# Scales of the weights spread over three other elements of distance attention; its last element interleaved with ratio attention's first tile

## The reference

```
# 1: distance attention, 16 heads of 16, 257 keys for each batch element
scores = Q K^T / 4 - slope[head] * (query_pos - key_pos);  masked: -inf
e = exp(scores - max);  attn = e / (1 + sum(e));  x = x + (attn V) W_o
# 2: ratio attention among the 32 tokens of an element, causal
dot = q k^T;  scores = dot^2 / (|q|^2 + |k|^2 - 2 dot + 1e-6)
x = x + softmax(scores) v w_out + b_out
# 3: feed-forward on weights rounded to 4 bits, in blocks of 32:
s = max(max|w_block| / 7, 1e-12);  w = clip(round(w / s)) * s
```

## Time and profile before

| | us |
|---|---|
| median of 3 runs | 744.56 (742.48 to 746.54) |
| the profiled execution | 744.72 |
| its span, first to last instruction | 742.9 |
| mean granted TensorE clock in it | 0.934 of full speed |

### The profile page before, as it was taken

How to read it: one execution, slowest core, us unless ns; L and a number is a source line. 1 busy time by engine, 2 the same in 40 slices (tenths; PEclk the granted TensorE clock), 3 DMA queues, 4 the chain that set the end, 5 groups by cost and what they waited for, 6 DMA issues and landing times.

```text
span 742.9 us, 18871 instructions
## 1 busy us (share of the span) xinstructions
PE 640.5 (86%) x7075; PEld 482.5 (65%) x7075; DVE 467.4 (63%) x1335; ACT 367.0 (49%) x992; POOL 311.5 (42%) x458
## 2 busy tenths in 40 slices
PE   4779999999989699986985899988999776999990
PEld 3557777877766578753434687667887573777760
DVE  1577766776776568874398864558878875333330
ACT  1445646655655569754486642336666431222320
POOL 1316655656632469720000030136565513556641
PEclk9889999999999889977997799999999986999995
DMA  8623332333310000039100525438001022243434
GB/s 266 225 58 87 88 78 72 89 82 81 88 36 3 2 3 4 4 96 336 51 1 0 213 71 226 173 131 366 3 3 65 3 100 53 46 70 59 66 44 71
DMA packets 31705, 65.21 MB, mean 88 GB/s; under 512 B 5792, under 2 KB 21792, under 8 KB 29312
## 3 DMA queue, kind: packets, MB, share of 16 engines
q1 hardware_dynamic: 26016, 55.73, 22.9%
q0 software_dynamic: 4688, 7.18, 5.9%
q10 hardware_dynamic: 912, 1.10, 0.4%
HBM read 57.67 MB, written 7.37 MB: 88 GB/s over the span
## 4 chain that ended last, share of the span: by engine, by line
PE 60%; DVE 23%; issue 5%; ACT 5%; DMA 2%; SPq 2%; POOL 0%; DVEq 0%; ACTq 0%; POOLq 0%
PE psum L2649 7%; PE psum L491 7%; PE psum L483 4%; PE psum L2659 4%; PE psum L516 4%; PE psum L1504 3%; PE psum L1481 3%; PE psum L859 3%; DVE ff_peak L1522 2%; DVE s_sb L659 2%; PE psum L868 2%; PE psum L851 2%; PE psum L505 2%; PE psum L899 2%; DMA wn<-in_w_down 2%
## 5 line engine op out<-in xcount | busy, mean ns | idle before, releaser
L804 POOL TENSOR_SCALAR bias<-dist,cst 128x257 f32<-128x257 f32 x128 | 59.8, 486 | 83.0 <-DVE dist L650 64.1
L659 DVE CUSTOM_DVE_ANT_0 s_sb<-psum,bias 128x257 f32<-128x257 f32 x128 | 46.9, 423 | 39.5 <-PE psum L505 37.5
L422 ACT ACTIVATE prob<-s_sb,negm 128x257 f32<-128x257 f32 x128 | 65.6, 512 | 4.9 <-DVE negm L663 4.9
L483 PE MATMUL psum<-ctxT,shared 128*128 128x257 f32 x256 | 62.9, 389 | 3.1 <-DMA msk<-in_mask 3.1
L491 PE MATMUL psum<-shared,ctxT 128*128 128x256 f32 x256 | 63.7, 394 | 0.0
L2649 PE MATMUL psum<-ex_w,shared 128*128 x184 | 58.3, 460 | 0.6 <-ACT shared L2542 0.6
L411 ACT COPY kT<-psum 128x257 f32<-128x257 f32 x64 | 23.8, 371 | 70.4 <-PE psum L483 70.4
L1743 POOL TENSOR_TENSOR wn<-wn,cst 128x1 f32<-128x1 f32 x8 | 4.7, 589 | 120.7 <-DVE wn L1870 120.7
L516 PE MATMUL psum<-cst,prob 128*128 128x128 f32 x256 | 41.2, 284 | 15.6 <-DVE pT L681 11.4
L483 PEld LDWEIGHTS psum<-ctxT,shared 128*128 128x128 f32 x256 | 47.2, 195 | 9.4 <-issue 3.8
L491 PEld LDWEIGHTS psum<-shared,ctxT 128*128 128x128 f32 x256 | 48.3, 199 | 5.7
(11 more groups left out here) (358 smaller groups left out, 1629.5 us busy)
## 6 DMA issues: line engine op xcount, KB each, us to landing
ctxT<-in_ctx_T SPq DMA_DIRECT2D x32, 257.0 KB
ex_w<-in_w SPq DMA_DIRECT2D x1, 5632.0 KB, 18.4
kpos<-in_kpos SPq DMA_DIRECT2D x32, 128.5 KB
msk<-in_mask SPq DMA_DIRECT2D x32, 128.5 KB
near_turned<-in_ctx_T_tiles SPq DMA_DIRECT2D x4, 1028.0 KB
ff_used_up<-in_ctx_T_tiles SPq DMA_DIRECT2D x4, 1028.0 KB
near_rows<-in_ctx_tiles SPq DMA_DIRECT2D x4, 1024.0 KB, 8.2
ff_used_up<-in_ctx_tiles SPq DMA_DIRECT2D x4, 1024.0 KB, 6.1
```

The lines of the kernel that those rows point to most:

```text
L422: nc.scalar.activation(prob[n % 2][:, g, :], s_sb[n % 2][:, g, :], ACT.Exp, bias=negm[:, b, g:g + 1], accum_out=esum[t % 2][:, b, g:g + 1]) \
L483: ins = nc.tensor.matmul(kv[m][:, 0:SK], w["xa_k"][:, k, P * m:P * m + P], ctxT[n % BT][:, k, :], start=(k == 0), stop=(k == KT - 1))
L659: nc.vector.tensor_tensor_reduce(s_sb[n % 2][:, g, :], sc[g][:, 0:SK], bias[n % 2][:, g, :], 1.0, float("-inf"), ALU.add, ALU.max, mx[:, b ...
L804: nc.gpsimd.tensor_scalar(bias[n % 2][:, g, :], dist[n % 2][:], c.slope[:, g:g + 1], 1.0, ALU.mult, ALU.mult).then_inc(bias_ready, 1)
```

## The change

Two parts.

**Scales.** Each third of the weights has a semaphore of its own. `scales(0)`, `(1)`, `(2)` now stand in n = 2, 6, 7, after `distances(n+1)` and ahead of `combine` and `rows_max(n)`. POOL waits before each piece for the third that it needs.

**The handover.** The loops end at n = 31. Ratio attention's steps are cut into small functions, and the order around n = 31 and after it is written out. Tile 0 of ratio attention is turned into the bank of the queries and keys, since the other one still holds values in n = 31; the projected bias row goes to bank 3.

```diff
+        FINAL, SCALED_AT = N - BT, (2, BT + 2, BT + 3)
 sync:
-                sp.dma_start(wn[...], a[name]).then_inc(wn_loaded, 16)
+                sp.dma_start(wn[...], a[name]).then_inc(wn_loaded[n], 16)
 scalar, in the loop at n == N - 1, behind turned(n - 2):
+                    ratio.act_xT(act, 0)
 scalar, after the loop (now range(N)):
+            ratio.act_start(act)
+            ratio.act_qk(act, 0)
+            ratio.act_squares(act, 0)
+            ratio.act_xT(act, 1)
+            exps(N - 1, 0)
+            exps(N - 1, 1)
+            turned(N - 2)
+            exps(N - 1, 2)
+            exps(N - 1, 3)
+            ratio.act_scores(act, 0)
+            ratio.act_norm(act, 2)
+            ratio.act_qk(act, 1)
+            turned(N - 1)
             act.sem_inc(gone, 1)
-            for u in range(-1, SPLIT + 1):
+            ratio.act_xT(act, 2)
+            ratio.act_v(act, 0)
+            ratio.act_norm(act, 3)
+            for u in range(0, SPLIT + 1):
 tensor, in the loop at n == N - 1, behind turn_p(n - 2, 1):
+                    ratio.pe_turn(pe, 0)
 tensor, there behind values(n):
+                    ratio.pe_qk(pe, 0)
 tensor, after the loop (now range(N)):
+            turn_p(N - 2, 0)
+            ratio.pe_turn(pe, 1)
+            turn_p(N - 2, 1)
             pe.wait_ge(s_done, 4 * N)
-            ratio.pe(pe, -1)
+            ratio.pe_scores(pe, 0)
+            turn_p(N - 1, 0)
+            weighted(N - 2)
+            ratio.pe_qk(pe, 1)
+            turn_p(N - 1, 1)
+            ratio.pe_row(pe)
+            weighted(N - 1)
+            ratio.pe_turn(pe, 2)
+            ratio.pe_v(pe, 0)
             spread_over(NT - 1)
+            ratio.pe_turn(pe, 3)
+            ratio.pe_qk(pe, 2)
+            ratio.pe_scores(pe, 1)
+            ratio.pe_v(pe, 1)
             output(NT - 1)
-            ratio.pe(pe, 0)
+            ratio.pe_values(pe, 0)
 vector:
+                if n in SCALED_AT:
+                    scales(SCALED_AT.index(n))
+                if n == N - 1:
+                    ratio.norm_stats(dve, 2)
+                    ratio.norm_stats(dve, 3)
                 rows_max(n)
-                if 1 <= n < 4:
-                    scales(n - 1)
 vector, after the loop (now range(N)):
+            copy_turned(N - 2)
+            own_heads_of(2 * NT - 2)
+            copy_turned(N - 1)
+            ratio.dve_inverse(dve, 0)
+            denominators(NT - 1)
+            ratio.dve_row(dve)
+            own_heads_of(2 * NT - 1)
+            ratio.norm_stats(dve, 4)
             combine(NT - 1)
+            ratio.dve_off_maximum(dve, 0)
+            ratio.norm_stats(dve, 5)
+            ratio.dve_turn(dve, 0)
             add_output(NT - 1)
+            ratio.dve_inverse(dve, 1)
 gpsimd:
-                    if n == BT:
-                        pool.wait_ge(scales_ready, 3)
+                    pool.wait_ge(scales_ready, 3 * (n - BT) * PER // NBLK + 1)
 gpsimd, after the loop:
+            ratio.pool_keys(pool, 0)
+            for n in (2, 3):
+                ratio.root(pool, n)
+                ratio.shift(pool, n)
+            ratio.pool_keys(pool, 1)
+            ratio.pool_ratio(pool, 0)
```

More of the change, by code:

```diff
@@ L584, in _ @@
             pe.wait_ge(w_loaded["xa_o"], 16)
-            for n in range(N + 2):
+            for n in range(N):
                 t, b = n // BT, n % BT
@@ L592, in _ @@
                     keys(n, 1)
-                if n == N:
+                if n >= 2:
+                    turn_p(n - 2, 1)
+                if n == N - 1:
+                    pe.wait_ge(loaded["ratio"], 16 * len(GROUPS["ratio"]))
                     pe.wait_ge(k_done[1], N)
                     pe.wait_ge(spread_read, NT - 1)
[L596 to L603, removed]
+                    ratio.pe_turn(pe, 0)
+                if n > 0:
                     values(n)
-                if t < NT and b > 0:
+                if n == N - 1:
+                    ratio.pe_qk(pe, 0)
+                if b > 0:
                     o_bank_free(n)
@@ L749, in _ @@
             dve.wait_ge(x_loaded, 16)
-            for n in range(N + 3):
+            for n in range(N):
                 t, b = n // BT, n % BT
@@ L1034, in pool_start, with pool_keys, pool_ratio @@
             pool.wait_ge(marked, 2)
+        def pool_keys(pool, n):
+            pool.wait_ge(k_ready, n + 1)
+            at_least(pool, s_full, n - 1)
+            for m in range(KT):
+                ins = spread_heads(nc.gpsimd, kbd[n % 2][:, m, :, :, :], kT[:, m, :], c.head)
+            ins.then_inc(kbd_ready, 1)
+        def pool_ratio(pool, n):
+            pool.wait_ge(s_read, n + 1)
+            at_least(pool, p_ready, n - 1)
+            for i, half in enumerate(HALVES):
+                pool.wait_ge(inverse_ready, 2 * n + i + 1)
+                nc.gpsimd.tensor_tensor(num[n % 2][:, half, :], square[n % 2][:, half, :],
+                                        inverse[n % 2][:, half, :], ALU.mult).then_inc(ratio_ready, 1)
+                pool.wait_ge(ratio_ready, 2 * n + i + 1)
+                nc.gpsimd.tensor_tensor(num[n % 2][:, half, :], num[n % 2][:, half, :],
+                                        c.causal.unsqueeze(1).broadcast_to([P, NH // 2, SQ]), ALU.add) \
+                    .then_inc(masked_ready, 1)
         def pool_step(pool, u):
@@ L1044, in pool_step @@
             if there(u + 2):
[L1045 to L1050, removed]
-            if there(u + 1):
[L1052 to L1060, removed]
-                                            c.causal.unsqueeze(1).broadcast_to([P, NH // 2, SQ]), ALU.add) \
-                        .then_inc(masked_ready, 1)
+                pool_keys(pool, u + 2)
+            if there(u + 1):
+                pool_ratio(pool, u + 1)
         def act_own(act, n):
@@ L1121, in act_step @@
             if there(u + 1):
[L1122 to L1132 removed]
+                act_scores(act, u + 1)
+                act_v(act, u + 1)
+            if there(u + 4):
                 act_norm(act, u + 4)
@@ L1235, in dve_row, with dve_turn, dve_inverse @@
             dve.wait_ge(row_full, 1)
-            nc.vector.tensor_tensor(row[:], qk_bank[:, 0:D], w["ra_bo"][:], ALU.add).then_inc(row_ready, 1)
+            nc.vector.tensor_tensor(row[:], row_bank[:, 0:D], w["ra_bo"][:], ALU.add).then_inc(row_ready, 1)
+        def dve_turn(dve, n):
+            dve.wait_ge(p_ready, n + 1)
+            at_least(dve, o_full, n - 1)
+            turn_blocks(nc, pT[n % 2], prob[n % 2]).then_inc(pT_ready, 1)
+        def dve_inverse(dve, n):
+            dve.wait_ge(den_ready, n + 1)
+            for half in HALVES:
+                nc.vector.reciprocal(inverse[n % 2][:, half, :], inverse[n % 2][:, half, :]) \
+                    .then_inc(inverse_ready, 1)
         def dve_step(dve, u):
```

207 lines of the change are left out of this document (103 added, 104 removed).

## The result

The changed kernel takes 721.69 us (720.97 to 721.99, 4 runs) against 743.52 us (742.02 to 746.54, 4 runs) for the kernel before: a ratio of 0.9706 [0.9671, 0.9741]. Its profiled execution took 721.83 us (span 720.0, mean granted clock 0.946), 22.9 less than the 744.72 of before; 21.4 were forecast.

The account below looks back on a forecast made before the run. PE, busy 86% of the span, was taken as the bound, gaining only where it idles or runs at a lower clock. Sum: 744.72 - 12.3 (scales, net) - 9.1 (handover) = 723.3 us; own range 720.5 to 725.5.

Parts of the forecast that it names:

- Scales, start: Elements n = 1 to 4: with the scales moved, PE no longer waits 4.79 us for the copy; gain 13.0 us.
- Context late: Start: context elements 4 and 5, needed some 10 us earlier, could come late; cost taken as 0.
- The bound from the idle DMA engines at 36: Start: DMA engines idle in 36 to 37 us, so context elements 4 and 5 had landed by 36; cost 0.
- Scales of n = 6 and 7: DVE in n = 6 and 7: its waits for PE hide the scales except 0.7 us; bounds 0 and 4.8.
- The fear that all of `scales` stretches as L694 did: n = 6 and 7: scales beside busy POOL stretching by 0.48 / 0.17 would cost some 9 us more.
- Handover: Last scores of distance attention to ratio tile 0's weighing: reordering gains 9.2 us, 9.1 taken; bounds 6 and 11.7.
- The 4.1 us of half clock: Handover: PE's busy 25.09 us includes 4.1 added by half clock, so 21.0 at full speed.
- A: Handover: clock falls at 243.6 and 251.5, gain only 5 to 6 instead of 9.1; 727 us; chance 0.15.
- D: Handover and next slot: TensorE stays at 1.2 GHz, costing +27; 750 us, slower than before; chance 0.03.
- The rest at nothing: Ratio attention's loop and all later stages just move with the earlier gain; cost or gain 0.
- B: Start: context 4 or 6 comes late, PE idles some 3 us in n = 4, clock falls; 728 us; chance 0.07.
- C: Start: moving the scales doesn't help, only the handover is gained; 735 to 736 us; chance 0.05.

Follow-up runs that it names:

- e5: Changed kernel with the scales in the same elements 2, 6, 7, but behind rows_max(n): 730.34 us, ratio 0.9805.
- e2: Changed kernel with the scales back behind the maxima of n = 1, 2, 3 and one semaphore for the three loads (handover part alone): 730.23 us, ratio 0.9813.
- e11: Changed kernel without the computing of the scales, constants written in their place: 721.17 us, ratio 0.9706.
- e1: Kernel before with the scales part of the change alone, its handover untouched: 730.32 us, ratio 0.9802.
- e3: Changed kernel with the last output projection back right behind spread_over(7) on PE: 724.48 us, ratio 0.9736.

## Why the prediction came out right

- **Scales, start: right.** Maxima of n = 2, 3, 4 were forecast at 31.3, 37.1 and 43.0 and stand at 29.61, 35.30 and 41.00; with n = 1 itself 1.67 earlier that is 31.3, 37.0 and 42.7 on the clock of before. The clock from 20 to 66 us is 1.00. e5 shows the cause as it was argued, the copy behind the scales. The size, 13.0 forecast and 13.3 measured from n = 1 to n = 4, hangs on the half clock in the profile of the kernel before, 3.1 us of which e2 did not have. What the prediction missed is that a wait with a fixed end (28.68) had been hiding any earlier begin of n = 1, so the 1.67 came on top. The begin itself varies between runs of these kernels (22.97 to 24.85), so a single profile can be that much off.
- **Context late: right, with less to spare than thought.** Element 4 landed at 33.9, and DVE waited 1.23 us for it; PE's scores came 0.32 after the distances were done. The bound from the idle DMA engines at 36 had room for this.
- **Scales of n = 6 and 7: right in size.** 0.7 forecast, 0.5 measured (e11). The reduce took 1.75 us beside POOL as without it; L768 took 0.29 to 0.36 instead of 0.19, and in all three elements it ended within 0.04 us of POOL's biases; in e5, with POOL idle beside it in n = 6 and 7, it took 0.19. The Trainium skill (SBUF — State Buffer, "Who interferes with whom") says that the reduce does not contend with GpSimd, while a `tensor_scalar` can; this trace agrees, with 1.75 us and with 0.29 to 0.36. The fear that all of `scales` stretches as L694 did would have cost some 9 us.
- **Handover: right.** 9.2 us forecast for the first weighing, 9.5 measured; idle times of 1.5 and 0.95 forecast, 1.51 and 0.97 measured; the end of the first weighing forecast 21.3 us after the last scores, 21.14 measured. The second weighing came 24.25 us earlier, the first 23.97: the 0.1 to 0.3 set aside for the reciprocals of tile 1 were not lost there, but the third came only 23.89 earlier. The 4.1 us of half clock in the forecast's sum are those of one execution: e1, with the same idle times, had 1.5 less.
- **The clock (rivals A and D): did not come.** After idle times of 1.51, 0.97 and, in e3, 1.95 us in the handover it stayed at 1.00.
- **The rest at nothing: wrong by +1.3 and -2.4.** This is the one step that failed. The prediction took all later stages for the same work at a fixed distance. They are the same work, but not at the same clock: full speed at the end of ratio attention (+1.94, of which 1.3 are left after small losses), and half speed longer in the feed-forward layer (-2.4).
- **Rivals B and C: did not come.** C falls with e1, whose gain is the start's.

The net of the three terms not forecast, +1.7, +1.3 and -2.4, is 0.6 us, and the two parts gave 0.5 and 0.4 more than their 12.3 and 9.1: that the forecast was as near as 1.5 us owes something to the cancelling of the three. It also owes something to the execution that it was made against, 744.72 us: at 737.56, the fastest run of the kernel before, the same run of the changed kernel would have gained some 7 us less.

## What to carry to other kernels

Look for work that stands between a result and the copy which another engine waits for, and move it to where its own engine would sit idle for that other engine anyway: the same 2.4 us cost 1.9 to 3.8 us more in each element behind the maxima than ahead of them, where all three together cost 0.5. At a change of stage, write out the order of each engine and ask of each long instruction who is queued behind it. And when a change shifts all later stages, expect a microsecond or two either way from the clock in stages it does not touch.

## What the runs showed of the hardware that was not expected

The half clock after an idle time can last a different time over the same instructions: after the same idle time of 5.10 us, with the same matmuls behind it, it was back at full clock by 345.04, the start of the projections, in the kernel before, and only 2.4 us after their start in the changed one. Idle times near 2 us went both ways, too. In e5, 1.97 at 35.10 was followed by a granted clock of 0.65 up to 40.00 (the values took 3.06 us), 2.29 at 73.75 by 0.68 up to 79.00, and 2.89, the longest, at 64.71 by 1.00 up to 69.00 (values 1.89). In the handover 1.66 us was followed by half clock in the kernel before and by full clock in e1. The length of an idle time alone does not tell what the clock will do.

A `tensor_tensor` on DVE with two operands in SBUF took 0.82 us (L751 at 240.38) beside a busy POOL. At its seven other places it took 0.42 or 0.43, and at 54.27 POOL was busy too, so that POOL is the cause is not shown.
